# Wider one-hots, an earlier edge factor and attention sums kept in PSUM, in a four-layer graph network

## The chip, the cores and the metric

The kernel runs on one core of a Trainium2 chip, as one program. The metric is the device time of one execution in microseconds (us), lower is better; it is given as the median of several executions.

## What is computed

A graph of 1250 nodes with 512 features, 20000 directed edges (sorted by target), an 8-valued edge type, a 2-valued edge type and an edge weight go through four layers. Each layer's result is added to its input and the rows are normalised. The reference, cut to what matters here:

```python
# layer 0: edge convolution
out = segment_sum(relu(concat([x[src], x[dst]], 1) @ W.T + b), src)
# layer 1: attention with 8 heads of 64, h = (x @ W.T).reshape(n, 8, 64)
e = leaky_relu(e_src[src] + e_dst[dst], 0.2)     # e_src = (h * a_src).sum(-1), e_dst alike
e = e * (1.0 + et_emb[edge_type_8])              # the edge factor, first half
e = e * edge_weight[:, None]                     # the edge factor, second half
e = exp(e - e_max[dst]); alpha = e / e_sum[dst]
out = segment_sum(h[src] * alpha, dst)           # the attention sums
# layer 2: x @ W_self.T + mean_over_neighbours(x) @ W_neigh.T
# layer 3: two gated layers with two relations, whose weights are mixed from 30 basis matrices each
w = einsum('rb,bio->rio', att, basis); agg = segment_sum(sigmoid(x_j @ gate_w) * x_j @ w[r], row)
```

## The kernel before

Nodes lie in NB = 10 blocks of 128 rows (the last partly padding). The edges are first ordered on the chip: a rank is worked out for each edge with one-hot matrices and matmuls, then each edge is written to its slot. Slots come in tiles of 128 edges, and two tiles that add to the same node block make a pair: 192 tiles (96 pairs) by source, 176 tiles (88 pairs) by target. In the order by target the last pairs hold nothing but padding, and their gathers read row 0.

The program is a row of stages, each its own block of five engine programs, with a barrier at its end (`stage_semaphores`, L44, sets up the semaphores). No engine starts a stage before all have left the last one. Inside a stage each engine has a hand-written order, and semaphores count what is done. The stages in time, with the lines of their functions:

- load, then `bucket_edges` (L452), 9 to 54 us.
- `place_edges` for the sources (L554), 54 to 166 us. For each of 160 tiles of 125 edges VectorE builds a one-hot of the partition (L586) and one of the slot times the packed value (L588), TensorE multiplies them (L599) into one PSUM bank. Beside it `Basis` (L169) loads 16 pieces of 2 MB of the first basis (L197), TensorE mixes them (L211), ScalarE copies them out (L220) and stores them.
- `sort_edges` for the targets (L233), 171 to 294 us: VectorE computes counts and ranks, among them which block a pair belongs to (up to L395), and then a gather loop waits for TensorE (L400).
- `count_edges` (L738), 298 to 483 us. It counts edges between node pairs per relation, in 192 tiles: VectorE builds a one-hot of the source within its block (L783, 128 wide) and one of the target (L784, 1280 wide), in f16. TensorE takes the PSUM bank and the turn of each tile from registers, which it loads for 8 tiles at a time, and multiplies in three matmuls of up to 512 columns (L805). ScalarE empties a bank (L826) and clears it (L815). GpSimd in the meantime writes 120 of the 160 columns of the by-target slots with indirect scatters, one `DMA_INDIRECT` per column (L627).
- `store_counts` (L832), 483 to 551 us: the counts are turned on TensorE and stored, VectorE adds two relations (L874), GpSimd issues the other 40 scatters.
- `node_stage` n0 (L1058), 566 to 648 us: per node block a copy of x (L2154), four transposes (L1160), 16 matmuls (L1171), and VectorE adds the bias (L1130) and splits the result in two parts (L1133, L1136, L1137). GpSimd has nothing to do in it. TensorE runs one block ahead of what VectorE finishes: two buffers each for the input block and for the result.
- `edge_convolution` e0 (L893), 648 to 927 us, and node stage n1, 927 to 985 us.
- `edge_scores` (L1643), 986 to 1159 us, in 11 steps of 4 groups of 4 tiles. VectorE builds one-hots for a group (L1718, twice) and a block mask (L1723), TensorE transposes them and looks up scores, VectorE multiplies by the mask (L1736) and reduces (L1744). The pieces of basis 2 are mixed in 8 of the 11 steps, from the second on. GpSimd works out the edge factor at the start: for each of 8 types a comparison (L1698), a product with the edge weight (L1699), a product with the embedding row (L1700) and, from the second type on, an addition (L1705).
- `attention_weights` (L1822), 1160 to 1205 us.
- `attention_pass` e1 (L644), 1206 to 1441 us. For each of 88 pairs GpSimd issues two gathers of 128 rows of h (L667, into 8 buffers), VectorE builds the one-hots (L689), multiplies the rows by the weights (L697) and, two pairs later, adds the sums of TensorE in PSUM to the block's accumulator in SBUF (L707, 512 wide, and L710, 9 wide). TensorE makes two pairs of matmuls per pair of tiles (L723, L725) into one of two banks in turn.
- the dense layers (L1387), 1441 to 2018 us: matmuls of layers 2 and 3 (L1333, L1381).

Of the kernel before, what the change touches and what calls it, by code (L numbers as in the profile page):

```python
# [23 lines left out]
P = 128  # L24
# [208 lines left out]
def sort_edges(nc, name, C, identb, key, packed, pair_block, block_f, pos_p, pos_s, value, address):  # L233
# [6 lines left out]
    with ExitStack() as ctx:  # L240
# [16 lines left out]
        eqtmp = sb("eq_tmp", [EP, 4, EP], F32)  # L257

# [94 lines left out]
        with ExitStack() as c1:  # L353
# [11 lines left out]
            def _(v):  # L365
# [29 lines left out]
                nc.vector.tensor_copy(block_f, pp[:, :])  # L395

# [157 lines left out]
def place_edges(nc, name, C, slots, pos_p, pos_s, value, sorted_out, basis):  # L554

    RING, STEP = 4, T // Basis.STEPS
    QUARTER = STEP // 4
    with ExitStack() as c1:
        sem = stage_semaphores(nc, c1, name)
        onp = c1.enter_context(nc.sbuf_tensor(f"{name}_onehot_p", [EP, RING, P], F32))  # L560
# [34 lines left out]
        def _(pe):  # L595
            def step(i, first=False, last=False):
                for u in range(STEP):
                    pe.wait_ge(built, i * STEP + (u + 1))
                    nc.tensor.matmul(po[:, 0:slots], onp[:, u % RING, :], ons[:, u % RING, :],  # L599
# [44 lines left out]
def attention_pass(nc, name, C, table, idx, loc, pair_block, acc, weight, side):  # L644

    ns = H + 1
    with ExitStack() as ctx:  # L647
# [4 lines left out]
        ohr = sb("onehot_ring", [P, 4, 2, P], F32)  # L652
        pS, pN = ps("pS", [P, 2, D], F32), ps("pN", [P, 2, D], F32)
# [4 lines left out]
        summed, added, nadded = sem("summed"), sem("added"), sem("nadded")  # L658
# [3 lines left out]
        def _(pool):  # L662
            for j in range(PAIRS):
                q = j % BODYP
                wait(pool, summed, j + 1 - BODYP)
# [12 lines left out]

        @block.vector
        def _(v):  # L680
            nc.vector.memset(acc[:, :, :], 0.0).then_inc(zeroed, 1)
            nc.vector.memset(side[:, :, :], 0.0).then_inc(zeroed, 1)
            v.wait_ge(zeroed, 2)
# [3 lines left out]
            def build(i, u):  # L687
                wait(v, summed, i * BODYP + (u - 3))
# [12 lines left out]
            def accumulate(i, u):  # L701
                j = i * BODYP + u
                b = v.value_load(pair_block[0:1, bass.ds(j, 1)], min_val=0, max_val=NB - 1)
                v.wait_ge(summed, j + 1)
                wait(v, added, j)
                a = flat(acc[:, bass.ds(b, 1), :])
                nc.vector.tensor_tensor(a, pS[:, u % 2, :], a, ALU.add).then_inc(added, 1)  # L707
                wait(v, nadded, j)
                a = flat(side[:, bass.ds(b, 1), :])
                nc.vector.tensor_tensor(a, pN[:, u % 2, 0:ns], a, ALU.add).then_inc(nadded, 1)  # L710

            lagged(v, NSTEP, BODYP, [(0, build), (0, multiply), (2, accumulate)], last=1)

        @block.tensor
        def _(pe):
            def scatter(i, u):
                j = i * BODYP + u
                pe.wait_ge(built, j + 1)
                pe.wait_ge(weighted, j + 1)
                wait(pe, nadded, j - 1)  # L720
                wait(pe, added, j - 1)
                for s in range(2):
                    nc.tensor.matmul(pS[:, u % 2, :], ohr[:, u % 4, s, :], rows[:, u, s, :],  # L723
                                     start=s == 0, stop=s == 1)
                    ins = nc.tensor.matmul(  # L725
                        pN[:, u % 2, 0:ns], ohr[:, u % 4, s, :],
# [1538 lines left out]
```

## Time and profile before

| | us |
|---|---|
| Median of 3 runs | 2023.15 |
| Lowest and highest run | 2022.13, 2029.55 |
| The profiled execution | 2020.42 |
| Its span, first to last instruction | 2018.7 |
| TensorE busy in it | 1618.9 (80%) |
| VectorE busy | 1257.3 (62%) |
| ScalarE busy | 446.2 (22%) |
| GpSimd busy | 656.6 (33%) |
| Mean granted TensorE clock, share of full speed | 0.894 |

All times of instructions below are of that one profiled execution, in us from the first instruction of the span. A stage with its barrier is over when its last engine is done, so a busy share says nothing before one knows which engine ends the stage. In groups of instructions the number behind "x" is the count, then stand the busy us, the mean ns of one, and the idle time of the engine just before them with what ended it. DVE is VectorE, ACT is ScalarE, POOL is GpSimd, PE is TensorE (PEld its weight loads), SP is the engine that issues most plain transfers.

### The profile page before, as it was taken

How to read it: one execution, taken by the hardware profiler on the slowest of the kernel's cores; microseconds unless marked ns; L12 is line 12 of the kernel's file. 1: busy time of each engine (PE TensorE's matmuls, PEld its weight loads, DVE VectorE, ACT ScalarE, POOL GpSimd, SP SyncE). 2: the span in 40 equal slices, each digit the busy share in tenths (PEclk: the TensorE clock that was granted, in tenths of full speed). 3: DMA queues.
4: the chain of work that ended last, by engine and by line, in shares of the span. 5: the costliest groups of instructions: out<-in, count | busy, mean ns of one | idle time of the engine just before them, and what ended most of it. 6: DMA issues, size and time to landing. Idle time of an engine off the chain costs nothing. (4 is left out here: it accounts for less than half of the span.)

```text
span 2018.7 us, 28932 instructions
## 1 busy us (share of the span) xinstructions
PE 1618.9 (80%) x7565; PEld 983.6 (49%) x7566; DVE 1257.3 (62%) x2769; ACT 446.2 (22%) x831; POOL 656.6 (33%) x604
## 2 busy tenths in 40 slices
PE   0787857774398999998658718989498899999998
PEld 0456743333353555554435514555244644774486
DVE  8676769883333777775597778888784832112222
ACT  0112203332211555554224320000010021001100
POOL 0000008777701776660370007777432011000000
PEclk9996559997689999999759759999799999999999
DMA  0792003003821666672239317777303400540034
GB/s 23 299 334 74 0 19 96 2 1 120 286 75 53 209 202 187 187 166 48 116 129 356 141 52 210 211 209 209 92 0 99 131 0 0 180 153 0 0 117 142
DMA packets 76313, 248.92 MB, mean 123 GB/s; under 512 B 14885, under 2 KB 28566, under 8 KB 68314
## 3 DMA queue, kind: packets, MB, share of 16 engines
q1 hardware_dynamic: 38618, 147.10, 20.2%
q0 software_dynamic: 34560, 96.84, 18.0%
q10 hardware_dynamic: 3072, 4.20, 0.7%
q8 instruction: 33, 0.54, 0.1%
q14 instruction: 30, 0.25, 0.0%
HBM read 215.91 MB, written 32.00 MB: 123 GB/s over the span
## 5 line engine op out<-in xcount | busy, mean ns | idle before, releaser
L627 POOL DMA_INDIRECT tab_slots<-slot_words,slot_address x160 | 197.7, 1235 | 350.4 <-issue 346.5
L1333 PE MATMUL dense_pY<-weights,dense_xT_block 128*128 128x512 f32 x640 | 283.6, 600 | 0.0
L1381 PE MATMUL dense_pY<-parts,dense_number 128*128 128x512 f32 x1000 | 238.4, 400 | 7.3 <-DMA dense_number<-tab_edges_to 7.3
L922 POOL DMA_INDIRECT e_rows<-tab_q,idx_q x192 | 182.5, 951 | 176.8 <-SPq L899 100.3
L667 POOL DMA_INDIRECT e_rows<-tab_h,idx_h x176 | 166.5, 946 | 208.9 <-SPq L647 155.6
L723 PE MATMUL e_pS<-e_rows,e_onehot_ring 128*128 128x512 f32 x352 | 193.3, 638 | 33.5 <-DVE side L710 22.2
L1381 PEld LDWEIGHTS dense_pY<-parts,dense_number 128*128 128x128 f32 x1000 | 189.3, 190 | 55.1 <-DMA dense_number<-tab_edges_to 8.4
L1333 PEld LDWEIGHTS dense_pY<-weights,dense_xT_block 128*128 128x128 f32 x640 | 121.4, 193 | 142.9 <-issue 142.9
L995 PE MATMUL e_pS<-e_rows,e_onehot_f 128*128 128x512 f32 x384 | 181.4, 596 | 0.0
L805 PE MATMUL count_pA<-count_onehot_d,count_onehot_s 128*128 128x512 f16 (+1 forms) x576 | 123.6, 365 | 52.0 <-DVE count_onehot_d L784 44.7
L697 DVE TENSOR_TENSOR e_rows<-e_rows,e_pW 128x1024 f32<-128x1024 f32 x88 | 107.4, 1221 | 32.0 <-DMA e_rows<-tab_h,idx_h 31.4
L784 DVE TENSOR_SCALAR count_onehot_d<-count_iota,dst_of_src 128x1280 f16<-128x1280 f16 x192 | 125.4, 653 | 0.0
L939 DVE TENSOR_TENSOR e_rows<-e_rows,e_pP 128x1024 f32<-128x1024 f32 x96 | 117.2, 1220 | 7.8 <-DMA e_rows<-tab_q,idx_q 7.2
L1351 DVE SCALAR_TENSOR_TENSOR parts<-dense_pY,dense_gates,parts 128x512 fp32r<-128x512 f32 x40 | 28.2, 747 | 146.8 <-ACT parts L1343 146.8
L805 PEld LDWEIGHTS count_pA<-count_onehot_d,count_onehot_s 128*128 128x128 f16 x576 | 57.9, 100 | 117.4 <-issue 102.0
L1171 PE MATMUL n_pY<-weights,n_xT_block 128*128 128x512 f32 x240 | 109.4, 607 | 0.0
L725 PEld LDWEIGHTS e_pN<-edge_weights,e_onehot_ring 128*128 128x128 f32 x352 | 67.3, 191 | 85.2 <-issue 85.2
L1560 DVE TENSOR_TENSOR acc<-dense_pY,acc 128x512 f32<-128x512 f32 x20 | 13.8, 692 | 146.2 <-PE dense_pY L1381 146.2
L964 ACT ACTIVATE e_rows<-e_rows 128x1024 f32<-128x1024 f32 x96 | 101.6, 1058 | 5.8 <-DVE e_rows L939 5.8
L948 DVE TENSOR_TENSOR acc<-e_pS,acc 128x512 f32 x96 | 66.4, 692 | 58.3 <-PE e_pS L995 58.3
L995 PEld LDWEIGHTS e_pS<-e_rows,e_onehot_f 128*128 128x128 f32 x384 | 73.0, 190 | 55.9 <-issue 47.6
L599 PE MATMUL src_pO<-src_onehot_s,src_onehot_p 125*128 125x192 f32 x320 | 65.6, 354 | 32.3 <-DVE src_onehot_s L588 32.3
(304 smaller groups left out, 2589.8 us busy)
## 6 DMA issues: line engine op xcount, KB each, us to landing
basis_piece<-in_L_gnn_basis_pieces SPq DMA_DIRECT2D x32, 2048.0 KB, 8.0
dense_number<-tab_edges_from SPq DMA_DIRECT2D x20, 1280.0 KB, 5.5
tab_edges_from<-counts_turned SPq DMA_DIRECT2D x10, 1280.0 KB
tab_edges_to<-counts_total SPq DMA_DIRECT2D x10, 640.0 KB
dense_number<-tab_edges_to SPq DMA_DIRECT2D x10, 640.0 KB, 4.5
tab_w<-basis_wout ACTq DMA_DIRECT2D x128, 32.0 KB
weights<-tab_w SPq DMA_DIRECT2D x4, 1024.0 KB, 6.7
weights<-in_L_gnn_W_T SPq DMA_DIRECT2D x3, 1024.0 KB
```

Source lines behind the costliest of these rows:

```text
L627: pool.indirect_dma_start(self.table, bass.IndirectOffsetOnAxis(self.address[:, t:t + 1], 0), self.words[:, t, :], None).then_inc(self.pla ...
L667: pool.indirect_dma_start(rows[:, q, s, :], None, table, bass.IndirectOffsetOnAxis(idx[:, j * 2 + s:j * 2 + s + 1], 0)).then_inc(got[q], 16)
L697: nc.vector.tensor_tensor(r, r, pW[:, bass.ds(i * 16 + u * 2, 2), :].unsqueeze(3).to_broadcast([P, 2, H, DH]), ALU.mult).then_inc(weighted, 1)
L723: nc.tensor.matmul(pS[:, u % 2, :], ohr[:, u % 4, s, :], rows[:, u, s, :], start=s == 0, stop=s == 1)
L784: nc.vector.tensor_scalar(ohd[:, u % RING, :], iota[:, :], dst[:, bass.ds(t, 1)], None, ALU.is_equal).then_inc(built, 1)
L805: ins = nc.tensor.matmul(flat(pA[:, bass.ds(bank[u], 1), a:b]), ohs[:, u % RING, :], ohd[:, u % RING, a:b], start=False, stop=True, skip_g ...
L922: pool.indirect_dma_start(rows[:, q, s, :], None, q_table, bass.IndirectOffsetOnAxis(idx[:, j * 2 + s:j * 2 + s + 1], 0)).then_inc(got[q], 16)
L939: nc.vector.tensor_tensor(rows[:, u, :, :], rows[:, u, :, :], pP[:, u % 2, :, :], ALU.add).then_inc(summand, 1)
L995: ins = nc.tensor.matmul(pS[:, u % 2, :], ohf[:, u, s, :], rows[:, u, s, :], start=s == 0, stop=s == 1)
L1171: ins = nc.tensor.matmul(py[:, k, w, :], xt[:, k, c, :], weights[w][0][:, c, :], start=c == 0, stop=c == 3)
L1333: ins = self.nc.tensor.matmul(self.banks.at(g), self.xt[:, b % 2, c, :], weights[:, c, :], start=c == 0, stop=c == 3)
L1381: ins = self.nc.tensor.matmul(self.banks.at(self.first + b), self.number[:, b % 2, r * NB + k, :], self.parts[r][n][:, k, :], start=k == 0 ...
```

## The change

- Placing: the partition one-hots of 5 tiles are built in one operation (5 x 128 wide, a tensor-tensor comparison of two broadcast inputs), in two buffers; the slot one-hots stay one operation per tile.
- Counting: the source one-hots of 8 tiles are built in one f16 operation (8 x 128 wide), from a new f16 copy of `loc`; a loop body holds 16 tiles in place of 8. TensorE still loads its registers per 8 tiles.
- The edge factor, 32 operations on GpSimd and the transfer of the embedding, is moved from `edge_scores` to node stage n0. The transfer is now issued on GpSimd's queue, before it on SP's. The buffer of the factor lives from there to the attention weights.
- The attention pass: TensorE adds all pairs of a node block in one PSUM bank (no start flag). ScalarE clears the banks with copies of zeros, and at a block's end copies the sums to the accumulator and clears the bank again. VectorE's two additions per pair and the clearing of the accumulator are gone. TensorE reads turn and bank of 8 pairs into registers at a time and waits per pair for `emptied`. For that `sort_edges` gets six small VectorE operations.

```diff
 def place_edges(...)
+                    if u % TOGETHER == 0:
+                        wait(v, placed, i * STEP + (u - TOGETHER))
+                        nc.vector.tensor_tensor(
+                            onp[:, u // TOGETHER % 2, :, :],
+                            C.f("iota_p", EP).unsqueeze(1).to_broadcast([EP, TOGETHER, P]),
+                            pos_p[:, bass.ds(t, TOGETHER)].unsqueeze(2).to_broadcast([EP, TOGETHER, P]), ALU.is_equal)
                     wait(v, placed, i * STEP + (u + 1 - RING))
-                    nc.vector.tensor_scalar(onp[:, k, :], C.f("iota_p", EP), pos_p[:, bass.ds(t, 1)], None,
-                                            ALU.is_equal)
...
 def count_edges(...)
-    RING, U = 4, 8
+    RING, G, U = 4, 8, 16
+            nc.vector.tensor_copy(loc_lo[:, :], loc[:, :])
...
+                if u % G == 0:
+                    if not (isinstance(i, int) and i * U + u < U):
+                        v.wait_ge(done, i * U + (u + 1 - G))
+                    nc.vector.tensor_tensor(
+                        ohs[:, u // G, :, :], iota_lo[:, :].unsqueeze(1).to_broadcast([P, G, P]),
+                        loc_lo[:, bass.ds(t, G)].unsqueeze(2).to_broadcast([P, G, P]), ALU.is_equal)
                 wait(v, done, t + 2 - RING)
-                nc.vector.tensor_scalar(ohs[:, u % RING, :], iota_lo[:, :], loc[:, bass.ds(t, 1)], None, ALU.is_equal)
                 nc.vector.tensor_scalar(ohd[:, u % RING, :], iota[:, :], dst[:, bass.ds(t, 1)], None, ALU.is_equal
                                         ).then_inc(built, 1)
...
 def node_stage(...)
+        if beside:
+            @block.gpsimd
+            def _(pool):
+                beside.compute(pool)
...
+class EdgeFactor:
+    def compute(self, pool):
+        pool.dma_start(flat(embv[:, :, :]), self.emb.rearrange("t h -> (t h)").partition_broadcast(P)).then_inc(self.emb_in, 16)
...
 def edge_scores(...)
-        @block.gpsimd
-        def _(pool):
-            link = chain(pool, s_pool)
-            pool.wait_ge(emb_in, 16)
-            link(nc.gpsimd.tensor_scalar(flat(embv[:, :, :]), flat(embv[:, :, :]), 1.0, None, ALU.add))
-            for t in range(8):
-                link(nc.gpsimd.tensor_scalar(of_type[:, 0, :], types, float(t), None, ALU.is_equal))
-                link(nc.gpsimd.tensor_tensor(of_type[:, 1, :], of_type[:, 0, :], weight, ALU.mult))
-                link(nc.gpsimd.tensor_tensor(
-                    part[:, :, :] if t else factor[:, :, :],
-                    of_type[:, 1, :].unsqueeze(2).to_broadcast([P, SLOTS, H]),
-                    embv[:, t, :].unsqueeze(1).to_broadcast([P, SLOTS, H]), ALU.mult))
-                if t:
-                    link(nc.gpsimd.tensor_tensor(factor[:, :, :], factor[:, :, :], part[:, :, :], ALU.add))
...
 def attention_pass(...)
+            def clear(at):
+                nc.scalar.copy(pS[:, at, :], zero[:, :])
+                nc.scalar.copy(pN[:, at, 0:ns], zero[:, 0:ns]).then_inc(emptied, 1)
...
+            for b in range(NB):
+                end = act.value_load(block_end[0:1, b:b + 1], min_val=0, max_val=PAIRS)
+                act.wait_ge(summed, end + 1)
+                act.wait_ge(emptied, b + 1)
+                nc.scalar.copy(acc[:, b, :], pS[:, b % 2, :])
+                nc.scalar.copy(side[:, b, :], pN[:, b % 2, 0:ns]).then_inc(taken, 1)
+                act.wait_ge(taken, b + 1)
+                clear(b % 2)
...
-            lagged(v, NSTEP, BODYP, [(0, build), (0, multiply), (2, accumulate)], last=1)
+            lagged(v, NSTEP, BODYP, [(0, build), (0, multiply)])
...
+                for u in range(BODYP):
+                    j = i * BODYP + u
+                    pe.wait_ge(emptied, turn[u] & 15)
+                    pe.wait_ge(built, j + 1)
+                    pe.wait_ge(weighted, j + 1)
+                    for s in range(2):
+                        nc.tensor.matmul(flat(pS[:, bass.ds(bank[u], 1), :]), ohr[:, u % 4, s, :], rows[:, u, s, :],
+                                         start=False, stop=True, skip_group_check=True)
```

## Rows read from the trace of the kernel before

**Rows 1.** The table by stretch (stretch, length, busy us by engine, clock, DMA share, GB/s).

```profile
54.00:165.00 111.00, 96.63 (x576) 58.21 (x576) 81.93 (x321) 19.42 (x32) 0.00 (x0) 1.00 0.85 321
299.00:483.00 184.00, 123.56 (x576) 57.87 (x576) 147.88 (x396) 58.01 (x126) 144.70 (x120) 0.91 0.18 32
566.00:648.00 82.00, 75.95 (x200) 35.55 (x200) 24.62 (x50) 10.96 (x20) 0.00 (x0) 0.96 0.08 32
995.00:1051.00 56.00, 28.67 (x294) 17.52 (x295) 56.00 (x43) 11.02 (x13) 53.71 (x29) 0.50 0.29 109
1060.00:1122.00 62.00, 53.89 (x804) 32.17 (x800) 45.65 (x120) 30.02 (x40) 0.00 (x0) 1.00 0.94 356
1206.00:1441.00 235.00, 201.64 (x704) 112.24 (x704) 199.24 (x354) 1.75 (x4) 166.48 (x176) 0.98 0.69 197
1441.00:2018.00 577.00, 531.10 (x1760) 325.09 (x1760) 226.78 (x502) 61.19 (x153) 50.67 (x40) 0.96 0.22 74
```

**Rows 2.** Groups of instructions, 995 to 1052 us (count, busy us, mean ns, idle before).

```profile
L1718 DVE TENSOR_TENSOR scores_onehots<-const_table,loc_dst 128x512 bf16<-128x512 f32 x8 | 24.8, 3100 | 0.0
L1705 POOL TENSOR_TENSOR edge_factor<-edge_factor,scores_factor_part 128x1408 f32<-128x1408 f32 x7 | 24.4, 3482 | 0.6
```

**Rows 3.** The line L1736, 1000 to 1052 us (ns min/median/max, first, last start).

```profile
L1736 DVE TENSOR_TENSOR scores_of_own_block<-scores_pLook,scores_onehot_block x7: 475/476/477, 1003.4 to 1051.2; 128x320 f32<-128x320 f32 x7
```

**Rows 4.** The same line where pieces of basis 2 stream in.

```profile
L1736 DVE TENSOR_TENSOR scores_of_own_block<-scores_pLook,scores_onehot_block x26: 480/481/484, 1056.6 to 1133.9; 128x320 f32<-128x320 f32 x26
```

**Rows 5.** The same line once no piece is left.

```profile
L1736 DVE TENSOR_TENSOR scores_of_own_block<-scores_pLook,scores_onehot_block x8: 480/482/483, 1140.0 to 1158.2; 128x320 f32<-128x320 f32 x8
```

**Rows 6.** Timeline of TensorE in node stage 0 (start us, us).

```profile
591.93 0.60 PE L1160 MATMUL n_pT<-const_table,n_x_block 128*128 128x128 f32 x4
...
599.24 0.60 PE L1160 MATMUL n_pT<-const_table,n_x_block 128*128 128x128 f32 x4
```

**Rows 7.** Groups of VectorE in node stage 0.

```profile
L1130 DVE TENSOR_TENSOR n_tmp<-n_pY,vectors 128x512 f32<-128x512 f32 x10 | 6.9, 692 | 52.1 <-PE n_pY L1171 52.1
L1137 DVE TENSOR_TENSOR p_low<-n_tmp,n_upper_bits 128x512 f32 (+1 forms) x10 | 6.8, 685 | 0.0
L1133 DVE TENSOR_SCALAR n_upper_bits<-n_tmp 128x512 int32<-128x512 int32 x10 | 4.3, 428 | 0.3
...
L2154 DVE COPY n_x_block<-x 128x512 f32 (+1 forms) x10 | 4.1, 423 | 6.6 <-PEq L50 5.6 <-PE n_pT L1160 1.0
```

**Rows 8.** The scatters of the count stage (columns as in rows 3).

```profile
L627 POOL DMA_INDIRECT tab_slots<-slot_words,slot_address x120: 1182/1187/2089, 298.8 to 478.8; - x120
```

**Rows 9.** Timeline of GpSimd in the stage behind it.

```profile
493.50 2.41 POOL L627 DMA_INDIRECT tab_slots<-slot_words,slot_address  x1 [0.30 <-issue]
```

**Rows 10.** Timeline of VectorE there.

```profile
493.36 1.49 DVE L874 TENSOR_TENSOR counts_total<-counts 128x1280 fp32r<-128x1280 f32 x1 [3.19 <-DMA tab_edges_from<-counts_turned]
```

**Rows 11.** Groups of the count stage.

```profile
L784 DVE TENSOR_SCALAR count_onehot_d<-count_iota,dst_of_src 128x1280 f16<-128x1280 f16 x192 | 125.4, 653 | 0.0
```

**Rows 12.** Timeline of TensorE in the count stage.

```profile
343.63 4.91 PE L805 MATMUL count_pA<-count_onehot_d,count_onehot_s 128*128 128x512 f16 x24 [1.87 <-DVE count_onehot_d L784]
```

**Rows 13.** The gathers of the attention pass.

```profile
L667 POOL DMA_INDIRECT e_rows<-tab_h,idx_h x176: 942/946/1042, 1206.8 to 1425.6; - x176
...
DMA to landing us min/median/max: 3.3/3.7/6.0
```

**Rows 14.** Groups of the attention pass.

```profile
L723 PE MATMUL e_pS<-e_rows,e_onehot_ring 128*128 128x512 f32 x352 | 193.3, 638 | 33.5 <-DVE side L710 22.2 <-DVE e_rows L697 9.0 <-issue 0.8
...
L697 DVE TENSOR_TENSOR e_rows<-e_rows,e_pW 128x1024 f32<-128x1024 f32 x88 | 107.4, 1221 | 32.0 <-DMA e_rows<-tab_h,idx_h 31.4
```

**Rows 15.** Timeline of TensorE in the attention pass.

```profile
1248.91 1.10 PE L723 MATMUL e_pS<-e_rows,e_onehot_ring 128*128 128x512 f32 x2
...
1249.98 1.10 PE L723 MATMUL e_pS<-e_rows,e_onehot_ring 128*128 128x512 f32 x2
```

**Rows 16.** A one-hot group of the placing stage.

```profile
L586 DVE TENSOR_SCALAR src_onehot_p<-const_table,pos_partition 125x128 f32<-125x128 f32 x160 | 45.3, 283 | 29.1 <-PE src_pO L599 27.5 <-DVEq L50 1.1
```

More of the change, by code:

```diff
@@ L641, with attention_pass @@
 NSTEP = PAIRS // BODYP
[L644 removed]
+def attention_pass(nc, name, C, table, idx, loc, block_turn, block_bank, block_end, acc, weight, side):
     ns = H + 1
@@ L687, in build @@
             def build(i, u):
-                wait(v, summed, i * BODYP + (u - 3))
+                if not (isinstance(i, int) and i * BODYP + u < 4):
+                    v.wait_ge(summed, i * BODYP + (u - 2))
                 nc.vector.tensor_tensor(
@@ L712, in _ @@
-            lagged(v, NSTEP, BODYP, [(0, build), (0, multiply), (2, accumulate)], last=1)
+            lagged(v, NSTEP, BODYP, [(0, build), (0, multiply)])
         @block.tensor
         def _(pe):
[L716 to L726, printed above, removed]
-                        weight[:, bass.ds(i * 16 + (u * 2 + s), 1), :].rearrange("p a h -> p (a h)"),
-                        start=s == 0, stop=s == 1)
-                ins.then_inc(summed, 1)
@@ L731, in _, with step @@
-            lagged(pe, NSTEP, BODYP, [(0, scatter)], last=1)
+            pe.sem_inc(summed, 1)
+            def step(i):
+                group = bass.ds(i * BODYP, BODYP)
+                _, turn = nc.values_load_multi_w_load_instructions(
+                    block_turn[0:1, group], (mybir.EngineType.PE,), min_val=1, max_val=NB,
+                    skip_runtime_bounds_check_because="a sum of as many comparisons")
+                _, bank = nc.values_load_multi_w_load_instructions(
+                    block_bank[0:1, group], (mybir.EngineType.PE,), min_val=0, max_val=1,
+                    skip_runtime_bounds_check_because="a single bit")
+                for u in range(BODYP):
[6 more added lines that the diff above has]
+                                         start=False, stop=True, skip_group_check=True)
+                        ins = nc.tensor.matmul(
+                            flat(pN[:, bass.ds(bank[u], 1), 0:ns]), ohr[:, u % 4, s, :],
+                            weight[:, bass.ds(i * 16 + (u * 2 + s), 1), :].rearrange("p a h -> p (a h)"),
+                            start=False, stop=True, skip_group_check=True)
+                    ins.then_inc(summed, 1)
@@ L1058, in node_stage @@
 def node_stage(nc, name, X, ident, prepare, n_stats, weights, save, targets, narrow=None,
-               keep_xT=None, ahead=None):
+               keep_xT=None, ahead=None, beside=None):
     nw = len(weights)
@@ L1093, in node_stage @@
         begun, went_ahead, s_pool = sem("begun"), sem("went_ahead"), sem("pool_waited")
+        if beside:
+            beside.begin(ctx, sem)
         block = ctx.enter_context(nc.Block())
@@ L1643, in edge_scores @@
 def edge_scores(nc, name, C, identb, est, edt, src_lo, src_block, loc, pair_block, es_out, ed_out,
-                emb, types, weight, factor, basis):
+                basis):
     U = 4
```

120 lines of the change are left out of this document (74 added, 46 removed).

## The prediction

> **What bounds the kernel now.** With a barrier behind each stage I first ask which engine ends each, so I begin with the table by stretch [rows 1]. The dense layers, from 1441 us, are TensorE's (531.10 of 577 us busy) and not touched. TensorE also ends node stage 0, with 75.95 of 82 us busy; there GpSimd does nothing and VectorE works 24.62 us. In the count stage, 299 to 483 us, VectorE is busy 147.88 us, but the list of scatters shows that GpSimd issues one every 1.51 us up to the end: (478.8 - 298.8) / 119 [rows 8]. In the first third of the scores stage, 995 to 1051 us, VectorE and GpSimd are both full and TensorE idles at a granted clock of 0.50. In the attention pass the gathers start every 1.25 us, (1425.6 - 1206.8) / 175, which is 2.50 us a pair of tiles and 20.0 us for 8 pairs [rows 13]. VectorE is as busy as TensorE there, and yet waits 31.4 us for gathered rows [rows 14].
>
> **The edge factor out of the scores stage.** The groups at 995 to 1052 us [rows 2] show one-hots of 512 elements at 3100 ns, while an operation of 512 elements with two SBUF inputs takes 685 ns in node stage 0, where GpSimd is idle (L1137) [rows 7]. GpSimd's L1705 beside them takes 3482 ns. So VectorE's operation lies there until GpSimd's ends, and then passes one. L1736, which reads PSUM, keeps its 476 ns beside GpSimd [rows 3] and after it [rows 4, 5]. The line L1736 runs once per group, so its starts give the pace: (1051.2 - 1003.4) / 6 = 7.97 us a group with the factor [rows 3], (1133.9 - 1056.6) / 25 = 3.09 us where pieces of basis 2 stream in [rows 4], where the DMA share is 0.94 [rows 1], and (1158.2 - 1140.0) / 7 = 2.60 us without either [rows 5]. Seven intervals are slow. Three lie ahead of the first mixing and come down to 2.60, four to 3.09: 3 x 5.37 + 4 x 4.88 = 35.6 us. The first group is held once too, 3.10 - 0.69 = 2.4 us. I take -37, a little less because the first slow interval is shorter. Bounds: -30, if groups keep 3.5 us at the clock of 0.50, and -40. What is late next is the stream of pieces, already in the 3.09. On SP's queue the embedding's transfer went ahead of the first piece; its absence is worth nothing, since that piece is first used four groups later.
>
> **The factor in node stage 0.** GpSimd's chain is 8 rounds of 7.97 us less one addition of 3.5, and some 3 us for the transfer and the first operation: 63 us from 566 on. The stage lasts to 648, so its end is covered, and the transfer on GpSimd's queue has nothing behind it but this chain. But the DVE operations there are the kind that was held: per block L1137 has two SBUF inputs (685 ns), and L1133, its twin L1136 and the copy L2154 are SBUF-to-SBUF (428 and 423) [rows 7]. L1130 reads PSUM. Behind the wait of VectorE stand the transposes of the next block: TensorE's budget is 599.24 - 591.93 = 7.31 us a block [rows 6]. If each of the four lets one GpSimd operation pass, a block lasts one GpSimd round. Of the 7.97 us some 1.5 were VectorE's passing (two one-hots at 0.69 and a small mask), so 6.4 to 7.0 are GpSimd's own; with the four at 1.97 us in all that is 8.4 to 9.0. I take 8.8, +1.5 us on each of some 6.4 blocks that the chain spans: **+10**. Bounds: 0, if the double buffers take it up (VectorE has 57 us free), and 7.97 + 1.97 = 9.9 us a block, +17. The Trainium skill's rule fits the held rows: the page "SBUF — State Buffer", section "Who interferes with whom", has one port pair shared by VectorE and GpSimd, given to one of them for a whole instruction. It speaks against this move, and by it the +10 is due rather than the 0; no row of before shows it in this stage.
>
> **One-hots of 8 tiles in counting.** GpSimd's scatters end the stage, so the time that VectorE saves (8 operations, a window in the loop) and TensorE's branch are worth 0. TensorE's gap for register loads, 1.87 us before 24 matmuls [rows 12], stays. What counts is whether the scatters stay at 1.51 us. In the next stage a scatter that begins at 493.50 takes 2.41 us [rows 9] instead of 1.187 [rows 8], just while L874, two SBUF inputs and 1.49 us, runs from 493.36 [rows 10]: it ends 1.06 us behind the L874. The new operation has two SBUF inputs as well. The nearest in size, L697 of 1024 elements, takes 1.22 us [rows 14]. A window of 1.2 us that falls anywhere on a scatter's cycle of 1.51 delays it by 1.2 x 1.2 / 2 / 1.51, less some 0.1 for the part without effect: 0.38 us, 24 times 9.1. The present excess of the 120 scatters over their median (a maximum of 2089 ns [rows 8]) was 2 us at most, and half may go with the removed operations: **+8**. L784 itself is stalled (653 mean [rows 11]) and stays so, without effect. Bounds: -2, if nothing is held, and +24, if each of the 24 holds a scatter for a full microsecond.
>
> The Trainium skill's page "VectorE: DVE Perf Modes", section "The perf-mode tier table (the rule you actually need)", lets a tensor-tensor operation on 16-bit SBUF data handle two elements at once, which would halve the new operation and is rival (c); but it asks that elements lie side by side, and one input here repeats a single element. No row of before has such an operation.
>
> **The attention pass.** VectorE loses two additions per pair, and TensorE the wait for them (22.2 us in all [rows 14]). But the gathers set the pace, and they wait only for free row buffers, so cover is GpSimd's 20.0 us per 8 pairs. TensorE needs 2 x (1249.98 - 1248.91) = 2.14 us a pair [rows 15], 17.1 for 8, and with a register gap as in counting, 1.87 [rows 12], 19.0: under 20.0, by one microsecond. ScalarE was busy 1.75 us in the stage [rows 1] and takes ten evacuations. The memset of the accumulator lay under the first gathers (3.7 us to land [rows 13]). At the end one wait and addition go, one copy out and a clear come. I take **-0.5**; bounds -2, that tail at its best, and +4, some groups at 20.4 us.
>
> **The small ones.** Placing: the stage streams pieces at a DMA share of 0.85 with TensorE at 96.63 of 111 us, GpSimd idle [rows 1]; five operations of 283 ns [rows 16] become one of about 0.8. What VectorE saves (0.6 per 5 tiles) is hidden by TensorE and the pieces: 0, bounds -2 and +2. Sorting: six operations, two of 880 elements on one partition (about 1.05 each, by L697's 1.22 for 1024) and four at 283 or so: 3.2 us ahead of a gather loop in which VectorE waits for TensorE. I take +0.5 of 0 to +3.2.
>
> **The sum** on the profiled execution: 2020.4 - 37 + 10 + 8 - 0.5 + 0 + 0.5 = 2001.4. The median of the runs is 2.7 above that execution, so 2004.
>
> **Rivals.**
>
> (a) Nothing is held in either new place: the double buffers absorb node stage 0, and the scatters slip between the wide operations. For it: VectorE is only 30% busy there. Against it: rows 2 and rows 9, 10. Terms 0 and -2: 1984 to 1986; say 1986.
>
> (b) One of the two bites: without node stage 0's +10 it is 1994, and with counting at its lower bound of -2 in place of +8 it is 1994 too.
>
> (c) The new operation handles two elements at a time, in half of L697's time, 0.61 us. Then a scatter is held by 0.61 x 0.61 / 2 / 1.51 = 0.12, less some 0.05, 24 times 2 us: 1998. For it: its data are 16 bits wide, L697's 32. Against it: the repeated element.
>
> (d) Both bite at their upper bounds, +17 and +24: 2004 + 7 + 16 = 2027, within the band of no change.
>
> (e) Slower: TensorE becomes the bound of the attention pass. Place: its 8 pairs with the register gap against 20.0 us. It decides from (20.0 - 1.87) / 8 = 2.27 us a pair. If the granted clock fell to a mean of 0.80 once its waits turn into gaps (it is 0.91 in the count stage, which has such gaps, and 0.98 here [rows 1]), a pair is 2.68 and 8 pairs 23.3: 11 x 3.3 = +36, 2040. Against it: there are fewer idle stretches than now.
>
> (f) The change does not do what it says in the scores stage: the seven groups stay at some 5 us because TensorE at half clock [rows 1], not the held operations, sets them. The gain is 7 x 2.97 + 2.4 = 23 in place of 37: 2018. Against it: TensorE is busy for 28.67 / 7 = 4.1 us a group there, mixing included.
>
> **Chances.** About 0.5% (10 us) is what a measurement of this kernel can tell. Forecast 0.41 (own range 1997 to 2012), (a) 0.20, (b) 0.13, (c) 0.03, (d) 0.14, (e) 0.06, (f) 0.03. Faster by over 0.5% (under 2013): 0.41 + 0.20 + 0.13 + 0.03 = 0.77; same: (d) and (f), 0.17; slower: (e), 0.06. The range goes from 1985 to 2018: it takes (a) and (f) in, and (d) and (e), 0.20, are left out.
>
> **What would show it.** Right: L1718 at 685 ns from the first group and the scores stage 35 to 38 us shorter; node stage 0 with blocks of 8.4 to 9.0 us and L1137 at over 2 us while GpSimd works; in counting, scatters of up to 2.3 us, about 16 of them, and a stage 8 us longer; gathers at 1.25 us unchanged, and the attention pass the same to 1 us. Wrong: node stage 0 of 82 us or a count stage of 184 (rival a); the new 1024-wide operation under 0.8 us (c); TensorE without idle time in the attention pass and gathers waiting for it (e); L1736 more than 4 us apart in the scores stage (f).

## The result and the profile after

| | before | after |
|---|---|---|
| Median of 5 runs, us | 2023.15 | 2007.86 |
| Lowest and highest | 2020.95, 2029.55 | 2004.50, 2010.74 |
| Profiled execution, its span | 2020.42, 2018.7 | 2010.74, 2009.0 |

The ratio is 0.9922, with a 95% interval of 0.9901 to 0.9944: faster by 0.8%, or 15 us, where 19 were forecast (2004). The profiled executions differ by less, 9.7 us (2020.42 and 2010.74): that of before is below all five of its runs, that of after is one of the two slowest of its five. So stages are compared and not only spans. A stage's length here is the time from one barrier to the next, read from GpSimd's last step in each barrier:

```
stage            before   after   difference   forecast
placing           116.8   112.1      -4.7         0
sorting by target 124.4   125.9      +1.5        +0.5
counting          185.1   206.9     +21.8        +8
storing counts     68.0    70.1      +2.1         0
node stage 0       82.6    82.5      -0.1       +10
scores            174.1   142.2     -31.9       -37
attention pass    235.1   235.5      +0.4        -0.5
dense layers      577.1   577.2      +0.1         0
```

The other stages differ by under 1 us. So a forecast that was near in the sum was far off in two of its terms, and these two cancel. The table by stretch of after, to be held against [rows 1]:

```profile
296.00:500.00 204.00, 120.12 (x576) 56.52 (x576) 138.30 (x229) 58.00 (x126) 166.62 (x120) 0.86 0.16 29
587.00:669.00 82.00, 75.89 (x200) 35.56 (x200) 49.66 (x50) 10.96 (x20) 55.28 (x33) 0.96 0.09 33
1007.00:1148.00 141.00, 116.50 (x1664) 76.66 (x1664) 102.60 (x273) 60.67 (x76) 0.00 (x0) 0.84 0.67 254
1196.00:1431.00 235.00, 203.71 (x704) 112.59 (x704) 137.14 (x177) 16.18 (x48) 166.92 (x176) 0.98 0.71 197
```

In counting, VectorE works less than before (138 us for 148) and the stage is longer, because GpSimd's 120 scatters are busy 166.6 us for 144.7. In node stage 0 VectorE is busy twice as long (49.66 for 24.62), and TensorE, which ends the stage, does not notice.

**Counting.** The scatters of after, in the view of [rows 8]:

```profile
L641 POOL DMA_INDIRECT tab_slots<-slot_words,slot_address x120: 1175/1350/2172, 296.0 to 497.8; - x120
```

The median rose from 1187 to 1350 ns. The timelines of GpSimd and VectorE in after show two kinds of holds:

```profile
348.51 2.17 POOL L641 DMA_INDIRECT tab_slots<-slot_words,slot_address  x1 [0.31 <-issue]
350.99 1.49 POOL L641 DMA_INDIRECT tab_slots<-slot_words,slot_address  x1 [0.30 <-issue]
```

```profile
347.76 0.74 DVE L819 TENSOR_SCALAR count_onehot_d<-count_iota,dst_of_src 128x1280 f16<-128x1280 f16 x1
348.42 1.20 DVE L815 TENSOR_TENSOR count_onehot_s<-count_iota_lo,count_loc_lo 128x1024 f16<-128x1024 f16 x1
349.55 2.34 DVE L819 TENSOR_SCALAR count_onehot_d<-count_iota,dst_of_src 128x1280 f16<-128x1280 f16 x4
```

The scatter at 348.51 begins as the new operation L815 runs and takes 2.17 us. That is the hold that the prediction priced. The one at 350.99 begins in a run of 1280-wide one-hots and takes 1.49. Before, the same place looked like this, GpSimd and then VectorE:

```profile
346.19 1.21 POOL L627 DMA_INDIRECT tab_slots<-slot_words,slot_address  x1 [0.30 <-issue]
347.70 1.20 POOL L627 DMA_INDIRECT tab_slots<-slot_words,slot_address  x1 [0.30 <-issue]
```

```profile
346.10 0.23 DVE L783 TENSOR_SCALAR count_onehot_s<-count_iota_lo,loc_src 128x128 f16<-128x128 f16 x1
...
346.88 0.81 DVE L784 TENSOR_SCALAR count_onehot_d<-count_iota,dst_of_src 128x1280 f16<-128x1280 f16 x1
347.61 0.23 DVE L783 TENSOR_SCALAR count_onehot_s<-count_iota_lo,loc_src 128x128 f16<-128x128 f16 x1
```

Both scatters begin as the short one-hot L783 runs, and are not held. It is the other way about: L784 waits for the scatter (0.81 us for its usual 0.54), and by that the two engines fall in step. I went through all 120 scatters of each trace and noted which operation of VectorE ran as each began, with at least 0.05 us to go, and by how much the scatter passed 1.187 us; "held" is by 0.1 us or more:

```
scatters that begin while ... runs       before           after
128-wide one-hot                         80, 0 held       (is gone)
1280-wide one-hot                        11, 3 held       60, 46 held, 13.9 us
1024-wide operation                      -                16, 14 held, 9.8 us
none of them                             29, 3 held       44, 2 held, 0.6 us
```

The same list gives the price of a hold. Of the 60 scatters of after that a one-hot or the wide operation held, 44 end 1.04 to 1.06 us behind the end of the operation that they met (15 more 1.2 to 1.3 us behind it), whether that one had 0.3 or 1.1 us left. One that is not held takes 1.18 us. So a hold costs what is left of the operation that is met, less 0.13 us: an estimate from these two figures, by which the short one-hot (234 ns at its shortest, with 145 ns left as the scatter at 347.70 begins) costs next to nothing.

### The profile page after: what moved, and what is told of

It reads as the page before. It is cut to its first block and busy times, and to the rows that moved or that the text cites. A ratio compares the mean times of both kernels' runs of the same rounds, so it can differ in the third digit from the quotient of the medians.

```text
span 2009.0 us, 27770 instructions
## 1 busy us (share of the span) xinstructions
PE 1613.5 (80%) x7565; PEld 985.0 (49%) x7566; DVE 1162.7 (58%) x2303; ACT 460.9 (23%) x875; POOL 677.8 (34%) x605
## 3 DMA queue, kind: packets, MB, share of 16 engines
q1 hardware_dynamic: 38474, 147.06, 20.2%
## 5 line engine op out<-in xcount | busy, mean ns | idle before, releaser
L641 POOL DMA_INDIRECT tab_slots<-slot_words,slot_address x160 | 221.5, 1384 | 347.7 <-issue 343.8
L727 DVE TENSOR_TENSOR e_rows<-e_rows,e_pW 128x1024 f32<-128x1024 f32 x88 | 107.5, 1221 | 92.2 <-DMA e_rows<-tab_h,idx_h 92.2
L819 DVE TENSOR_SCALAR count_onehot_d<-count_iota,dst_of_src 128x1280 f16<-128x1280 f16 x192 | 110.5, 616 | 18.0 <-PE count_pA L841 16.4
```

What stands on the lines that cost most here:

```text
L641: pool.indirect_dma_start(self.table, bass.IndirectOffsetOnAxis(self.address[:, t:t + 1], 0), self.words[:, t, :], None).then_inc(self.pla ...
L727: nc.vector.tensor_tensor(r, r, pW[:, bass.ds(i * 16 + u * 2, 2), :].unsqueeze(3).to_broadcast([P, 2, H, DH]), ALU.mult).then_inc(weighted, 1)
L819: nc.vector.tensor_scalar(ohd[:, u % RING, :], iota[:, :], dst[:, bass.ds(t, 1)], None, ALU.is_equal).then_inc(built, 1)
```

## Experiments

Each expectation names its own theories, and a letter can mean another thing in another run. On counting (e1, e2, e5, e6), **A** is that a scatter is held by whatever long operation on SBUF runs on VectorE as it begins, and that the short one-hots used to give it its place; **B** and **C** are that the wide operation alone does it, or the amount of VectorE's work. **D** and **E** are on node stage 0, **F** and **G** on the attention pass. Ratios are to the kernel before on the same chip (medians there 2019.69 to 2022.03).

**e1: the new counting alone.** `count_edges` of after, all else as before.

> The kernel before with only the new count stage. In the profile of after, the count stage is 206.9 us long against 185.1 before, and 62 of its 120 scatters are held: 8 by 0.98 us beside the 1024-wide operation and some 54 by 0.31 us beside the 1280-wide one. Theory A (any operation of VectorE that runs as a scatter starts holds it; the short one-hot per tile used to give the scatters a place to start): the stage is 207 us here too, and the whole is 20 to 24 us slower than before, about 2045. Theory B (only the 1024-wide operations hold scatters, the rest of the 22 us is a matter of that one execution or of what the other parts changed ahead of it): the stage is 193 us and the whole 2031.

Measured: 2044.63 us, ratio 1.013 (1.0112 to 1.0147), counting 209.1 us. 65 scatters were held, for 26 us. The change of counting is a loss of 23 to 26 us by itself. (The 8 holds beside the wide operation that the expectation counts are those of some 0.98 us in after; with the shorter ones there are 14, as in the table above.)

**e2: everything but counting.** `count_edges` of before in the kernel after.

> The changed kernel with the count stage of before. Theory A: count stage 185 us, store stage back by up to 2 us, the whole 22 to 24 us faster than the changed kernel, 1984 to 1988 and 1.8% under before. Theory B: 8 us faster than the changed kernel, 2000.

Measured: 1985.86 us, ratio 0.9827 (0.9812 to 0.9842), counting 184.3 us, storing 67.4. These are theory A's numbers; B is out.

**e3: the edge factor alone.** `EdgeFactor` beside node stage 0, all else as before.

> The kernel before with only the edge factor moved to node stage 0. Theory A (node stage 0 has room, since VectorE's held operations end before TensorE needs the next block; the scores stage gains 32 us): node stage 0 82.5 us, scores stage 142 us, the whole 1991. Theory B (the move costs something elsewhere, as in the weights stage or in the gathers of the edge convolution, and part of the 32 us seen came from the other parts): over 1996.

Measured: 1983.50 us, ratio 0.9823 (0.9808 to 0.9838). Node stage 0 is 82.0 us, scores 140.6 against 174.1 before. This one edit is all of the gain, and more: 36 to 38 us, of which 33.5 in the scores stage. I had expected 1991. The scores stage gave 1.5 us more than expected; the largest part of the rest lies in placing, which the edit does not touch (113.1 us here, 116.8 in the profile of before).

**e4: the attention pass alone.** New `attention_pass` and `sort_edges`.

> The kernel before with only the attention pass that keeps its sums in PSUM, with the small operations in the sort. Theory A (the gathers set the pace): attention pass 235 to 236 us against 235.1, sort up to 2 us longer, the whole 2023 to 2026. Theory B (TensorE and VectorE were part of the bound): attention pass 5 us or more shorter, the whole under 2019.

Measured: 2023.96 us, ratio 1.0015 (1.0006 to 1.0025): the pass 234.6 us, sorting 125.8 against 124.4. That is a loss of some 3 us (1 to 5 by the interval), of which 1.4 is in the sort.

**e5: the 1024-wide one-hot reads its places from PSUM.** Kernel after, with

```diff
-        loc_lo = sb("loc_lo", [P, SRC_SLOTS], F16)
+        loc_lo = ctx.enter_context(nc.psum_tensor(f"{name}_loc_lo", [P, D], F32))
-            nc.vector.tensor_copy(loc_lo[:, :], loc[:, :])
+            nc.vector.tensor_copy(loc_lo[:, 0:SRC_SLOTS], loc[:, :])
```

> The changed kernel, its 1024-wide one-hot with the source's place read from PSUM in place of SBUF, so that it has only one input in SBUF. Theory A (a scatter is held by whatever operation with two SBUF inputs, or one-input SBUF-to-SBUF operation, is running as it starts): the 8 holds of 0.98 us go, the holds of 0.31 beside the 1280-wide one-hot stay, 55 to 75 of them; count stage 196 to 202 us. Theory C (the 1024-wide operation is the whole cause, and the holds of 0.31 follow from it): the stage goes back to 185.

Measured: 1995.58 us, ratio 0.9874 (0.9859 to 0.9889), some 10 us faster than after by the two ratios. Counting takes 195.8 us. The line of its scatters, and in the groups of instructions that of its wide operation:

```profile
L641 POOL DMA_INDIRECT tab_slots<-slot_words,slot_address x120: 1172/1182/1715, 297.0 to 487.6; - x120
```

```profile
L815 DVE TENSOR_TENSOR count_onehot_s<-count_iota_lo,count_loc_lo 128x1024 f16<-128x1024 f16 x24 | 29.0, 1207 | 0.0
```

The operation is as long as before (1207 ns), and 12 scatters began beside it, of which 1 was held, for 0.2 us. 60 began beside the 1280-wide one-hot, and 44 of them were held (I had expected 55 to 75), for 12.3 us in all. So one edit of the operand takes the first kind of hold away and leaves the second. The edit also makes the operand f32 where it was f16, which was not tried by itself; the time of the operation does not show it. The Trainium skill ("SBUF — State Buffer", section "Who interferes with whom") says that an operation with at most one input in SBUF, outside the modes that use two ports, does not contend with GpSimd. The run agrees, with 1 of 12 held in place of 14 of 16.

**e6: the short one-hot put back.** Kernel after, with a 128-wide one-hot into a spare buffer ahead of each wide one:

```diff
+                nc.vector.tensor_scalar(spare[:, u % RING, :], iota_lo[:, :], loc[:, bass.ds(t, 1)], None, ALU.is_equal)
                 nc.vector.tensor_scalar(ohd[:, u % RING, :], iota[:, :], dst[:, bass.ds(t, 1)], None, ALU.is_equal
```

> The changed kernel with the old 128-wide one-hot per tile put back ahead of each 1280-wide one, into a spare buffer that nobody reads; VectorE does more than before and more than after. Theory A (the short operation is what gives a scatter its place to start): the holds of 0.31 us go, those of 0.98 stay, count stage 190 to 197 us, shorter than 206.9 in spite of the added work. Theory C (more work of VectorE is more holding): 207 or longer.

Measured: 2003.48 us, ratio 0.9911 (0.9895 to 0.9926), counting 202.5 us: shorter than the 206.9 of after though VectorE does 192 operations more, but longer than the 190 to 197 that I expected. GpSimd and VectorE of this kernel:

```profile
345.64 2.21 POOL L641 DMA_INDIRECT tab_slots<-slot_words,slot_address  x1 [0.30 <-issue]
348.15 1.18 POOL L641 DMA_INDIRECT tab_slots<-slot_words,slot_address  x1 [0.30 <-issue]
349.63 1.18 POOL L641 DMA_INDIRECT tab_slots<-slot_words,slot_address  x1 [0.30 <-issue]
```

```profile
345.58 1.20 DVE L816 TENSOR_TENSOR count_onehot_s<-count_iota_lo,count_loc_lo 128x1024 f16<-128x1024 f16 x1
...
348.09 0.28 DVE L820 TENSOR_SCALAR count_spare<-count_iota_lo,loc_src 128x128 f16<-128x128 f16 x1
...
349.57 0.28 DVE L820 TENSOR_SCALAR count_spare<-count_iota_lo,loc_src 128x128 f16<-128x128 f16 x1
```

71 scatters began in a short one-hot and none of them was held; beside the 1280-wide one 4 were, for 1.1 us in place of 13.9. But being in step works against the stage once per 8 tiles: a scatter then begins while L816 runs, 21 times for 24 operations and mostly just as it begins, and is held for 0.9 us on average, 18.9 us in all for 9.8 in after. All 25 scatters that an operation held in this trace end 1.04 to 1.06 us behind it. More work of VectorE was not more holding, so C is out.

**e7: the factor moved, the addition of the store stage in five pieces.**

```diff
-                    nc.vector.tensor_tensor(total[:, b % 2, :], counts[:, b, 0, :], counts[:, b, 1, :], ALU.add
-                                            ).then_inc(added, 1)
+                    for c in range(0, NP, 2 * P):
+                        ins = nc.vector.tensor_tensor(total[:, b % 2, c:c + 2 * P], counts[:, b, 0, c:c + 2 * P],
+                                                      counts[:, b, 1, c:c + 2 * P], ALU.add)
+                    ins.then_inc(added, 1)
```

> The kernel before with the edge factor moved, and in the store stage the addition of 1280 elements (1.49 us, two SBUF inputs) cut into five of 256. Theory A: an addition of 256 lasts about 0.42 us and holds a scatter for 0.3 us at most, so of the 5.3 us of holds in that stage 3 to 5 go: store stage 64 to 66 us in place of 69.1, the whole 3 to 5 us under the kernel with the factor alone (1983.5). Theory C (five operations in a row hold as long as one): 69 us, no gain.

Measured: 1985.35 us, ratio 0.9809 (0.9795 to 0.9822), no gain that shows over e3 (the intervals overlap), where 3 to 5 us were expected. The holds did go. The scatters of this stage in e3, and then in e7:

```profile
L627 POOL DMA_INDIRECT tab_slots<-slot_words,slot_address x40: 1172/1182/2462, 478.5 to 543.1; - x40
```

```profile
L627 POOL DMA_INDIRECT tab_slots<-slot_words,slot_address x40: 1172/1181/1437, 486.8 to 545.6; - x40
```

From first to last they take 58.8 us in place of 64.6. But the stage only went from 69.1 to 68.0, since SP waits until 67.4 us into it for the last store of counts to land. That wait ended 1.5 us earlier in e3; why it is later here was not tried. So the holds did set the end of this stage, but the next bound lay 1 us behind them.

**e8: the factor moved, two more operations per block in node stage 0.**

```diff
+                    for e in range(2):
+                        nc.vector.tensor_tensor(more[:, e, :], tmp[:, :], upper[:, :].bitcast(F32), ALU.subtract)
                     nc.vector.tensor_tensor(low, tmp[:, :], upper[:, :].bitcast(F32), ALU.subtract
```

> The kernel before with the edge factor moved, and in node stage 0 two more operations of VectorE per block with two SBUF inputs (0.69 us each, into a spare buffer). Theory D (node stage 0 has room of about 1.3 us a block: VectorE's chain, with its one long hold, ends 5.9 us after the matmuls and the next block's transposes come 7.3 after): the added 1.4 us and the holds they draw go past it, blocks of 8.5 to 9.5 us while the chain lasts, node stage 0 at 90 to 96 us. Theory E (VectorE's free time in the stage, 30 us, takes it in): 82 to 83 us.

**e11: the same two operations without the factor.**

> The kernel before with the two more operations per block in node stage 0, without the edge factor there. Theory D (they cost only as they draw holds from GpSimd): node stage 0 stays at 82 to 83 us, the whole as before; with the factor beside them it was 104.9. Theory E' (the added work alone passes the budget of a block): 88 us or more.

Measured: e8 2007.64 us, ratio 0.993 (0.9915 to 0.9946), node stage 0 at 104.9 us, 23 more than in e3 and more than the 90 to 96 that I expected. e11: 2020.12 us, ratio 1.0009 (0.9998 to 1.0019), node stage 0 at 84.4, somewhat over the 82 to 83 expected. TensorE's transposes of two blocks in e8, to be read with [rows 6]:

```profile
587.06 1.12 PE L1170 MATMUL n_pT<-const_table,n_x_block 128*128 128x128 f32 x4 [5.20 <-DVE n_x_block L2175]
...
599.28 0.66 PE L1170 MATMUL n_pT<-const_table,n_x_block 128*128 128x128 f32 x4 [1.90 <-DVE n_x_block L2175]
```

Blocks last 12.2 us there (8.5 to 9.5 were expected), and TensorE waits for VectorE's copy. In the block from 599 us on, three of VectorE's operations meet a long one of GpSimd (of 3.22, 2.94 and 3.48 us). In after only one per block does, as shown further below.

```profile
599.86 2.67 DVE L1136 TENSOR_SCALAR n_upper_bits<-n_tmp 128x512 int32<-128x512 int32 x1
...
604.60 3.10 DVE L1142 TENSOR_TENSOR p_low<-n_tmp,n_upper_bits 128x512 f32 x1
607.63 3.37 DVE L2175 COPY n_x_block<-x 128x512 f32 x1
```

Two operations of 0.69 us cost 2 us in the whole stage alone, and 23 beside GpSimd's chain.

**e9 and e10: fewer gathers in the old and the new attention pass.** Both kernels leave out 80 of the 176 gathers, so their sums are not the attention's, and both have the factor moved: e9 too, where its expectation says "the kernel before". They are to be held against e3 (pass 234.6 us), not against before.

```diff
             for j in range(PAIRS):
                 q = j % BODYP
+                if j >= BODYP and q % 2:
+                    continue
...
-                v.wait_ge(got[u], (i + 1) * 32)
+                v.wait_ge(got[u], 32 if u % 2 else (i + 1) * 32)
```

> The kernel before, its attention pass with the gathers of every second pair left out from the ninth pair on (those pairs multiply the rows that lie in the buffer, so the sums are not the attention's). 176 gathers become 96. Theory F (the gathers set the pace of this pass): the pass goes from 235.1 to 210 to 222 us, VectorE's own 2.35 to 2.5 us a pair. Theory G (VectorE or TensorE set the pace and the gathers lie beside them): 230 us or more.

> The same gathers left out in the kernel with the edge factor moved and the new attention pass (placing and counting as before). Theory F: the pass goes from 234.5 to 205 to 215 us, TensorE's 19.0 us for 8 pairs, so that the new pass is 5 to 12 us shorter than the old one once the gathers do not bind. Theory G: as long as the old pass of e9, or longer, since the register gap and ScalarE's evacuation cost what VectorE saves.

Measured: the old pass 203.1 us (the kernel 1950.95), the new one 202.5 (the kernel 1952.10). Both are shorter by 32 us, more than expected (210 to 222 and 205 to 215), which is theory F for the bound: the gathers set it. But the new pass is 0.6 us shorter than the old, where 5 to 12 were expected. The pass in e9, and then in e10:

```profile
1164.00:1367.00 203.00, 193.66 (x704) 107.74 (x704) 194.60 (x354) 1.75 (x4) 90.69 (x96) 0.97 0.45 124
```

```profile
1170.00:1373.00 203.00, 193.46 (x704) 107.66 (x704) 136.55 (x177) 16.55 (x49) 90.78 (x96) 0.97 0.45 124
```

TensorE is busy 193.5 of 194 us between its first and last matmul in both, 2.20 us a pair. VectorE has 58 us less to do in the new pass and nobody waits for that. The register reads of the new pass leave no gap that shows.

**e12: the factor moved, the addition cut, and 117 scatters while counting.** `PLACED_WHILE_COUNTING = 117`.

> The kernel with the edge factor moved and the addition of the store stage cut into five, and 117 in place of 120 scatters placed while counting. In e7 GpSimd ended the store stage's scatters 4 us ahead of the last store to memory, so the three moved there fit in. Theory A: count stage 184.4 - 4.5 = 179.9, store stage 68 to 69, the whole 3 to 5 us under e7 and some 43 us under the kernel before. Theory H (the stage's transfers are also slowed by more scatters beside them): store stage 72 us, no gain.

Measured: 1979.61 us, ratio 0.9802 (0.9789 to 0.9815), counting 179.6 and storing 68.6 us. The stages came out as expected (179.9, and 68 to 69 us), 4 us less in their sum than in e7; the whole is 1.4 us under e7 by the two ratios, with intervals that overlap, where 3 to 5 were expected. It is the lowest median of the kernels that do the whole work, and by the two ratios 1.2% under the changed kernel. It has neither the new counting nor the new placing or attention pass.

## Why the prediction came out as it did

The sign and the range of the whole held, and the largest term rests on what was read from [rows 2 to 5]. Two middle terms were wrong by 10 and 14 us in opposite directions, so that the sum came near is luck. No rival had the pair that was measured, nothing in node stage 0 (rival a) and nearly the upper bound in counting (rival d); a node stage of 82 us was among the signs of being wrong. There is luck too in the step from the profiled execution to the median, +2.7 by before: against the profiled execution of after, 2010.74, the 2001.4 is off by 9.3 us, against the median by 4.

**The scores stage** gave 31.9 of 37 us, near the lower bound. The line L1736 is L1788 in after:

```profile
L1788 DVE TENSOR_TENSOR scores_of_own_block<-scores_pLook,scores_onehot_block x44: 480/481/481, 1015.4 to 1147.3; 128x320 f32<-128x320 f32 x44
...
L1788 DVE TENSOR_TENSOR scores_of_own_block<-scores_pLook,scores_onehot_block x13: 480/481/481, 1015.4 to 1054.8; 128x320 f32<-128x320 f32 x13
```

The seven slow intervals went from 55.3 us to 20.4, as the term had it (3 x 2.60 + 4 x 3.09 = 20.2). The first group is 1.5 us earlier, for 2.4. What the step left out are the five intervals behind them: 19.0 us, where they took 14.4 before. Half of that is the clock: here TensorE's granted clock is 0.72 from 1015 to 1036 us, and from 1036 to 1055 us it falls back to half twice, 0.82 in the mean. In e3 it stays at 1.00 from 1008 to 1027 us, and the same five intervals take 16.7 us (16.2 to 16.8 in the seven kernels with the factor moved whose clock does not fall back there, and 17.6 and 17.3 in e8 and e9, where it does once). The stretch in after, and then in e3:

```profile
1036.00:1055.00 19.00, 16.16 (x208) 9.37 (x208) 11.45 (x31) 8.47 (x11) 0.00 (x0) 0.82 0.89 342
```

```profile
1008.00:1027.00 19.00, 16.09 (x238) 9.50 (x239) 13.02 (x36) 8.72 (x12) 0.00 (x0) 1.00 0.92 346
```

The clock that falls back is also the main difference between the 142.2 us of the stage in this profile and the 140.6 in e3. The other 2.3 us stay at full clock. The fourth to sixth piece of basis 2 are being fetched meanwhile, where before the third and fourth had been fetched in the slow stretch (issued at 1021.4 and 1037.2 us); that they are the cause was not tried. Rival (f) is out: the first seven intervals are 4.0 us at most, at a granted clock of 0.72, and L1718 takes 684 ns from the first group on.

**Node stage 0**, +10 forecast and nothing measured: the step that failed is "If each of the four lets one GpSimd operation pass, a block lasts one GpSimd round", with VectorE's 1.97 us on top of that round. VectorE and GpSimd in one block of after:

```profile
606.11 0.69 DVE L1168 TENSOR_TENSOR n_tmp<-n_pY,vectors 128x512 f32<-128x512 f32 x1 [1.68 <-PE n_pY L1214]
606.84 0.43 DVE L1171 TENSOR_SCALAR n_upper_bits<-n_tmp 128x512 int32<-128x512 int32 x1
607.30 3.26 DVE L1174 TENSOR_SCALAR p_high<-n_upper_bits 128x512 fp32r<-128x512 f32 x1
610.48 0.81 DVE L1175 TENSOR_TENSOR p_low<-n_tmp,n_upper_bits 128x512 fp32r<-128x512 f32 x1
611.22 0.79 DVE L2209 COPY n_x_block<-x 128x512 f32 x1
```

```profile
606.99 3.29 POOL L1312 TENSOR_TENSOR edge_factor<-edge_factor,factor_part 128x1408 f32<-128x1408 f32 x1
610.37 0.70 POOL L1305 TENSOR_SCALAR factor_of_type<-types 128x176 f32<-128x176 f32 x1
611.15 0.57 POOL L1306 TENSOR_TENSOR factor_of_type<-factor_of_type,slots_dst 128x176 f32<-128x176 f32 x1
611.80 2.68 POOL L1307 TENSOR_TENSOR factor_part<-factor_of_type,factor_emb 128x1408 f32<-128x1408 f32 x1
```

Three of the four operations are held, but only one of them by a long operation of GpSimd; the next two meet its short ones (0.70 and 0.57), and then VectorE has nothing to do until the next block while the 2.68 runs. The chain ends at 612.00, and TensorE's next transposes are due at 613.22. A hold costs what is left of the *particular* operation that it meets. And GpSimd's rounds, where the prediction had 8.4 to 9.0 us, follow each other by

```profile
L1312 POOL TENSOR_TENSOR edge_factor<-edge_factor,factor_part x7: 3157/3219/3290, 599.2 to 644.6; 128x1408 f32<-128x1408 f32 x7
```

(644.6 - 599.2) / 6 = 7.57 us, and 7.50 from the third on. The round from 595.14 to 602.46 us, which VectorE hardly met, took 7.32. So GpSimd's own time is 7.3 us, where the prediction had 6.4 to 7.0, and letting VectorE's operations pass adds 0.2, where it had 1.97. The 7.50 are still more than a block of 7.31. The copy of each block ends 1.48 us ahead of TensorE's transposes at first, 1.21 in the block shown, and about 0.2 less with each further one, 0.43 at 642 us, where the chain ends. So the buffers took up the chain as it is and could have taken up about two more rounds (an estimate from these figures). e8 shows how little was to spare otherwise: two small operations more and the blocks are 12.2 us, past even the upper bound of 9.9. The rule of the Trainium skill that was cited there ("SBUF — State Buffer", section "Who interferes with whom") is borne out as to the holding, and did not decide the time.

**Counting**, +8 forecast and +21.8 measured. The term for the 1024-wide operation itself was right: 24 times 0.38 = 9.1, measured 9.8. So was the number of its holds, 14 where about 16 were named. What failed is "half may go with the removed operations": the removed short one-hots were what kept the scatters free of the 1280-wide ones, and without them came 46 holds of 0.30 us, 13.9 us. e5 and e6 take away one kind each. The prediction had looked at L784 only as the one that waits. The +21.8 lies within the bounds (-2 to +24), but by a cause that was not among the terms. Rival (c) is out: the f16 operation takes 1213 ns for 1024 elements per partition, as the f32 one of the same width does (L697, 1221 [rows 14]). That fits the condition in the Trainium skill ("VectorE: DVE Perf Modes", section "Mode 2×_1P — pack two bf16 into one 32-bit read") that two elements at a time must be neighbours, though no run here has the operation without the repeated element.

**The attention pass** and **placing** came out as argued, 0 to within 1 us. In the attention pass the reasons were half right: the gathers are the bound (176 from 1196.4 to 1415.7, 1.25 us each, as in [rows 13]), but the waits of TensorE for VectorE (22.2 us [rows 14]) were only slack that the gathers leave, and the register gap of 1.87 us is not there. Placing took 111.4 to 113.5 us in the profiles of eight further kernels with the old code and 120.5 in one (e7), and 111.1 to 113.5 in four with the new. So the 4.7 us in the first table come from the profiled execution of before, which took longer there than most, and not from the change. **Sorting** cost 1.5 us, within its bounds.

## What to carry to other kernels

Before an operation on VectorE is merged or removed, look at what the *other* engine starts beside it: a short operation may be the only place where GpSimd's next one can begin unheld. Here work for GpSimd cost nothing beside a stage in which TensorE sets the pace and VectorE's chain per block ends early (82.5 us with it and without it), because only one long operation met VectorE per block; measure that room rather than take VectorE's idle share for it. And in the one operation tried (e5), an input in PSUM in place of SBUF took the holds away at no cost in its own time (1207 ns for 1213).

## What was not expected of the hardware

- A hold works both ways and pulls the engines into step: before, 80 of 120 scatters began within the short one-hot, whose 192 instances are busy for 67 of the 185 us of the stage.
- A held scatter ends 1.04 to 1.06 us behind the operation of VectorE that it met, in 44 of 60 cases in after and all 25 in e6, however much of that operation was left.
- Two operations of 0.69 us per block cost 2 us in a stage of 82 when GpSimd is idle and 23 us when it has a chain of long operations beside it (e11, e8).
- In the attention pass TensorE reads 16 register values for each 8 pairs with no gap that shows (e10), while in counting it loses 1.87 us at such a place [rows 12]. Why was not tried; there the wait ended on VectorE's one-hot.
